# Three local edits in a fused feed-forward kernel: a sigmoid built from a tangent, one subtraction moved two products back, and the last additions cut in halves

## The chip, the cores and the metric

The kernel runs on one core of a Trainium2 chip, as one launch. The metric is device time in microseconds (us). Three runs of the kernel before took 884.63, 884.65 and 885.28 us (median 884.65).

Names used throughout: PE is the matrix engine (PEld its weight load), ACT the scalar engine, DVE the vector engine, POOL the engine that runs the remaining elementwise work, SP the engine whose queue issues nearly all transfers.

## The reference, cut to what matters

The input is 4096 tokens of 128 features. Layer 0 is a conditional mixture of experts followed by an eight-expert gated feed-forward; layer 1 is a second mixture (two shared experts, eight routed ones of which each token uses two) followed by a low-rank feed-forward. The change lies in layer 1 and in the last addition:

```python
# routing of layer 1, the "second choice" for half of the tokens
s = sigmoid(router_in @ W_router.T)              # tokens x 8
_, topk_idx = top_k(s + router_bias, 2)
denom = sum of s over the two chosen             # the "token sum"
gates = where(denom > 1e-9, s_sel / (denom + 1e-9), 0.5)
# routed experts
for e in range(8):
    h = gelu(x @ r_w1[e].T)                      # exact gelu
    routed += (h @ r_w2[e].T) * gates_full[:, e:e+1]
# low-rank feed-forward and residual
x = x + (gelu((x1 @ U1) @ V1 + b1) @ U2) @ V2 + b2
```

## The kernel before, in words

Tokens lie as eight blocks of 512 columns (b = 0 to 7), features across the 128 partitions. Every matrix product is made from a high part and a low part of its fp32 operands: the hidden value `Hf` is rounded to `HH` (fp32r), and `HL = Hf - HH` is the low part. A "down" product of a hidden tile takes one matmul with `HH` (line 973) and one with `HL` (line 975) in this part of the program.

The program is a list of items, one hidden tile of 128x512 each, walked by a slot number k. All engines are written out by hand in one loop over k, each in its own order; an item's "up" matmuls are issued in its slot and its "down" matmuls LAG = 5 slots later. In layer 1 the kinds are:

- S, a tile of a shared expert: six up matmuls (lines 933, 938, 952, two results), Silu on ACT into `Sg` (line 1087), product on DVE (line 1568);
- R, the routed expert `ex` of a block: three up matmuls, exact gelu in place in PSUM on ACT (line 1083), product with the token's gate on DVE (line 1575), which frees the PSUM bank;
- F, a tile of the low-rank feed-forward: one up matmul (line 908), gelu on ACT (line 1080).

Pairs of blocks are served together: S of both (8 tiles), F of the pair before (up to block 4), R of both (16 tiles). F of the blocks 5, 6 and 7 come last, behind R of block 7. Up results use four PSUM banks in turn; a matmul into a bank waits for what freed it four results ago.

In an R slot, rounding to `HH` is on ACT (line 1093), but on DVE for experts 3 and 7 (line 1585). The low part is on POOL (line 1683), but on DVE for experts 1 and 5 (line 1588), and for expert 7 of block 7. On DVE the product of slot k comes first and the rounding and the low part of the item of slot k-1 behind it. So the low part of expert 5 stands behind the product of expert 6.

The routing decision is `choose(g, step)`, spread over ten slots from `pick[g][0]` on; g = 1 (the second choice) starts at the first S tile of block 2, g = 0 earlier. In its first slot ACT takes the Sigmoid of `LR` (line 1047); DVE then finds the two largest of eight per token with 128x128 operations in PSUM and ends with sums, a reciprocal and two products (lines 1386 to 1404). PE transposes the result (line 878), DVE copies it (line 1407), SP writes it to `scratch`, and the gates of blocks 4 to 7 are read back from there.

At the end of a block ACT copies a PSUM result to `PH` (lines 1053, 1058), DVE makes `PS` (line 1545) or `QS` (line 1553) of it, PE multiplies `QS` by `V2S` (line 893), DVE adds bias and residual (line 1560), and SP sends the block out (line 748). Functions of ACT come in tables; a change of table is an instruction of its own, `ACT_TABLE_LOAD`.

## Time and profile before

| what | value |
|---|---|
| median of three runs | 884.65 us |
| the profiled execution | 884.92 us, its span 883.1 us |
| granted clock, mean over the span | 0.999 |
| PE busy | 869.6 us, 98% of the span |
| PEld, DVE, ACT, POOL busy | 78%, 77%, 65%, 46% |
| queue q1 (SP's transfers) | 82.15 MB, 30.4% of 16 engines' span |
| chain that ended last | PE 83%, DVE 6%, ACT 3%, issue 3% |

The span is from the first to the last record of the profiled execution; the rest of its 884.92 us lies around it. A row of the timeline gives the start, the duration, the engine with its line, the operation with what it writes and reads, and in brackets the idle time of the engine before it with what ended it. "x2" means two instructions merged.

### The profile page before, as it was taken

To read this page: it belongs to the slowest core of one execution; us is meant where nothing else is said; L and a number is where in the kernel's file an instruction comes from. 1 tells how busy PE (TensorE), PEld (TensorE's weight loads), DVE (VectorE), ACT (ScalarE), POOL (GpSimd) and SP (SyncE) were. 2 spreads that over 40 slices of the span, in tenths; PEclk is the share of its full clock that TensorE was granted. 3 is DMA by queue.
4 is the path that set the end of the run, shared out by engine and by line. 5 is a ranking of instruction groups with operands and counts; after the bars stand their busy time and mean duration, and the time that the engine had idled before them with its cause. 6 is when DMAs were issued, how large, how long until landed. Compare 5 with 4: busy or idle time off the path is not lost.

```text
span 883.1 us, 12612 instructions
## 1 busy us (share of the span) xinstructions
PE 869.6 (98%) x3838; PEld 691.1 (78%) x3838; DVE 678.7 (77%) x1091; ACT 573.8 (65%) x1031; POOL 407.5 (46%) x379
## 2 busy tenths in 40 slices
PE   9999999999999999999999999999999999999997
PEld 6788888777888888888888888888888887777773
DVE  7877777869689687686687686686665788998887
ACT  7888888765555455555555555555555678989795
POOL 7457783135356353252252252352324427755462
PEclk9999999999999999999999999999999999999999
DMA  9689880024113112012012012011010068482700
GB/s 313 223 277 312 290 296 32 1 86 135 49 48 111 36 48 84 1 47 84 1 49 83 1 49 84 0 48 49 1 47 1 1 131 201 99 174 56 159 25 36
DMA packets 36548, 83.23 MB, mean 94 GB/s; under 512 B 4480, under 2 KB 14592, under 8 KB 34688
## 3 DMA queue, kind: packets, MB, share of 16 engines
q1 hardware_dynamic: 36192, 82.15, 30.4%
q8 instruction: 31, 0.51, 0.2%
q14 instruction: 37, 0.30, 0.1%
q10 hardware_dynamic: 288, 0.26, 0.1%
HBM read 71.39 MB, written 6.83 MB: 89 GB/s over the span
## 4 chain that ended last, share of the span: by engine, by line
PE 83%; DVE 6%; ACT 3%; issue 3%; SPq 2%; DMA 2%; POOL 1%; DVEq 0%; ACTq 0%; POOLq 0%
PE ps L933 17%; PE ps L952 17%; PE ps L938 17%; PE ps L993 9%; PE ps L995 9%; PE ps L988 9%; DVE HL L1588 2%; SPq L658 1%; PE ps L975 1%; PE ps L973 1%; DMA TMP<-scratch 1%; DVE Hf L1575 1%; ACT HH L1093 1%; POOL HL L1683 1%; DVE Hf L1568 1%
## 5 line engine op out<-in xcount | busy, mean ns | idle before, releaser
L1087 ACT ACTIVATE Sg<-ps 128x512 f32<-128x512 f32 x288 | 171.7, 597 | 243.7 <-PE ps L952 243.1
L1568 DVE TENSOR_TENSOR Hf<-ps,Sg 128x512 f32<-128x512 f32 x288 | 198.0, 688 | 148.9 <-ACT Sg L1087 93.0
L1683 POOL TENSOR_TENSOR HL<-Hf,HH 128x512 fp32r<-128x512 f32 x135 | 181.1, 1348 | 170.4 <-ACT HH L1093 154.3
L1093 ACT ACTIVATE HH<-Hf 128x512 fp32r<-128x512 f32 x346 | 216.1, 625 | 19.0 <-DVE Hf L1568 12.7
L1588 DVE TENSOR_TENSOR HL<-Hf,HH 128x512 fp32r<-128x512 f32 x243 | 216.7, 892 | 4.4 <-ACT HH L1093 3.2
L933 PE MATMUL ps<-XHL,WBH 128*128 128x512 f32 x512 | 203.6, 398 | 1.6 <-DVE Hf L1568 1.5
L952 PE MATMUL ps<-XHL,WBH 128*128 128x512 f32 x512 | 202.1, 395 | 0.0
L938 PE MATMUL ps<-XHL,WBL 128*128 128x512 f32 x512 | 202.0, 395 | 0.0
L1698 POOL TENSOR_TENSOR XT<-XT,TMP 128x512 f32<-128x512 f32 x64 | 83.9, 1311 | 226.0 <-DVE TMP L1435 225.9
L933 PEld LDWEIGHTS ps<-XHL,WBH 128*128 128x128 f32 x512 | 96.0, 188 | 26.2 <-DVE Hf L1568 3.2
L952 PEld LDWEIGHTS ps<-XHL,WBH 128*128 128x128 f32 x512 | 96.0, 188 | 23.1
L938 PEld LDWEIGHTS ps<-XHL,WBL 128*128 128x128 f32 x512 | 96.2, 188 | 21.9
L993 PE MATMUL ps<-HH,WBL 128*128 128x512 f32 x256 | 101.0, 395 | 0.0
L988 PE MATMUL ps<-HH,WBH 128*128 128x512 f32 x256 | 100.7, 393 | 0.0
L995 PE MATMUL ps<-HL,WBH 128*128 128x512 f32 x256 | 100.7, 393 | 0.0
L1588 DVE TENSOR_TENSOR HL<-ps,HH 128x512 fp32r<-128x512 f32 (+1 forms) x116 | 69.7, 614 | 29.4 <-ACT HH L1093 28.3
L1080 ACT ACTIVATE ps<-ps,GWU 128x512 f32<-128x512 f32 (+1 forms) x84 | 49.2, 588 | 16.9 <-PE ps L952 16.8
L988 PEld LDWEIGHTS ps<-HH,WBH 128*128 128x128 f32 x256 | 48.0, 187 | 12.0 <-DVE TMP L1435 0.4
L993 PEld LDWEIGHTS ps<-HH,WBL 128*128 128x128 f32 x256 | 48.0, 188 | 11.8
L995 PEld LDWEIGHTS ps<-HL,WBH 128*128 128x128 f32 x256 | 48.1, 188 | 11.2
L933 PE MATMUL ps<-XHL,WCH 128*128 128x512 f32 x128 | 51.1, 399 | 1.2 <-ACT Sg L1087 0.8
L952 PE MATMUL ps<-XHL,WCH 128*128 128x512 f32 x128 | 50.5, 395 | 0.0
(261 smaller groups left out, 1327.8 us busy)
## 6 DMA issues: line engine op xcount, KB each, us to landing
CWB<-scratch SPq DMA_DIRECT2D x14, 1024.0 KB, 4.7
GWD<-expert_down SPq DMA_DIRECT2D x21, 576.5 KB, 4.5
GWU<-expert_up SPq DMA_DIRECT2D x21, 514.0 KB, 5.4
CWB<-scratch SPq DMA_DIRECT2D x40, 256.0 KB, 6.0
ST<-in_wb_dram SPq DMA_DIRECT2D x8, 768.0 KB, 6.6
ST<-scratch SPq DMA_DIRECT2D x24, 256.0 KB, 8.8
GX<-XT SPq DMA_DIRECT2D x68, 64.0 KB, 2.7
XT<-in_x_dram SPq DMA_DIRECT2D x8, 256.0 KB, 5.8
```

What stands on the lines that cost most here:

```text
L933: e.matmul(o, wh, tokens(it, 0), start=True, stop=False)
L938: e.matmul(o, wl, tokens(it, 0), start=False, stop=False)
L952: e.matmul(o, wh, tokens(it, 1), start=False, stop=True).then_inc(s_z, 1)
L988: e.matmul(bk[:, 0:n], wh, HH[:, hs, 0:n], start=it.new, stop=False)
L993: e.matmul(bk[:, 0:n], wl, HH[:, hs, 0:n], start=False, stop=False)
L995: e.matmul(bk[:, 0:n], wh, HL[:, hs, 0:n], start=False, stop=it.last).then_inc(s_down, 1)
L1087: e.activation(Sg[:, it.n % NG, :], zb[z % NZ][:, :], ACT.Silu).then_inc(s_act, 1)
L1093: e.activation(HH[:, it.n % NH, 0:it.cols], hidden_place(it), ACT.Copy).then_inc(s_hi_act, 1)
L1568: e.tensor_tensor(Hf[:, it.n % NS, :], zb[z % NZ][:, :], Sg[:, it.n % NG, :], ALU.mult).then_inc(s_prod, 1)
L1588: e.tensor_tensor(l, f, h.bitcast(F32), ALU.subtract).then_inc(s_lo_dve, 1)
L1683: e.tensor_tensor(HL[:, it.n % NH, :], Hf[:, it.n % NS, :], HH[:, it.n % NH, :].bitcast(F32), ALU.subtract).then_inc(s_lo_pool, 1)
L1698: e.tensor_tensor(XT[:, it.blk, :], XT[:, it.blk, :], TMP[:, t % 2, :], ALU.add).then_inc(s_acc, 1)
```

## The change

Four edits, all on ACT and DVE; PE, POOL and SP keep their instructions in their order.

1. The second choice's sigmoid is no longer one ACT instruction at the first S tile of block 2. ACT takes tanh(x/8) three slots earlier (`odds`), DVE makes 1/max(tanh+1, 1e-6) one slot later, ACT squares twice one slot after that, and DVE adds one and takes the reciprocal in the slot of that first S tile.
2. In both choices the token sum and two values made from it lie in PSUM (`total`, `above`) instead of the SBUF scratch `r0`, `r1`.
3. The low part of routed expert 5 (`low_after`) is written one slot later in DVE's order, behind the product of expert 7.
4. The last addition of block 6 is made in two halves of 256 columns, the first ahead of the last `QS`, the second in the old place.

```diff
+        odds = pick[1][0] - 3
+        y_half = {t_f[NBLK - 1] + 1: NBLK - 2}
...
+            it.low_after = it.kind == "R" and it.ex == 5 and not it.lo_pool
...
# ACT
+                if k == odds:
+                    e.wait_ge(*ab_done.of(("B", 7)))
+                    e.activation(pick_place(1)[0], LR[:, 16:32, 0:8], ACT.Tanh, scale=0.125).then_inc(s_odds, 1)
+                if k == odds + 2:
+                    e.wait_ge(s_score, 1)
+                    e.activation(pick_place(1)[1], pick_place(1)[0], ACT.Square, bias=1.0, scale=-2.0).then_inc(s_power, 1)
+                    e.wait_ge(s_power, 1)
+                    e.activation(pick_place(1)[0], pick_place(1)[1], ACT.Square).then_inc(s_power, 1)
...
# DVE, choose()
+                total, above = [ab_bank(("pick", g))[:, 384 + 16 * i:400 + 16 * i] for i in range(2)]
...
-                    link(e.tensor_reduce(r0[:, 0:16], sel, AX, ALU.add))
-                    after()
-                    link(e.tensor_scalar(r1[:, 0:16], r0[:, 0:16], 1e-9, None, ALU.add))
+                    link(e.tensor_reduce(total, sel, AX, ALU.add))
+                    after()
+                    link(e.tensor_scalar(above, total, 1e-9, None, ALU.add))
...
-                    link(e.tensor_tensor(r1[:, 0:16], r0[:, 0:16], r2[:, 0:16], ALU.mult))
+                    link(e.tensor_tensor(r1[:, 0:16], total, r2[:, 0:16], ALU.mult))
...
# DVE, the loop
+                if k == odds + 1:
+                    t = pick_place(1)[0]
+                    e.wait_ge(s_odds, 1)
+                    link(e.tensor_scalar(t, t, 1.0, 1e-6, ALU.add, ALU.max))
+                    after()
+                    e.reciprocal(t, t).then_inc(s_score, 1)
+                if k == odds + 3:
+                    t = pick_place(1)[0]
+                    e.wait_ge(s_power, 2)
+                    link(e.tensor_scalar(t, t, 1.0, None, ALU.add))
+                    after()
+                    link(e.reciprocal(t, t))
...
+                if k in y_half:
+                    b, c = y_half[k], slice(0, BLK // 2)
+                    e.wait_ge(*small.of(("y", b)))
+                    e.scalar_tensor_tensor(out=out_place(b)[:, c], in0=ab_bank(("y", b))[:, c], scalar=col("b2"),
+                                           in1=XT[:, b, c], op0=ALU.add, op1=ALU.add).then_inc(s_ab, 1)
...
+                if 2 <= k <= len(items) + 1 and items[k - 2].low_after:
+                    it = items[k - 2]
+                    e.wait_ge(*hi[it.n])
+                    e.tensor_tensor(HL[:, it.n % NH, :], hidden_place(it), HH[:, it.n % NH, :].bitcast(F32),
+                                    ALU.subtract).then_inc(s_lo_dve, 1)
...
-                    if not it.lo_pool:
+                    if not (it.lo_pool or it.low_after):
```

The order of ACT around the second choice, in block 1 (`ps<-ps` is a gelu, `ps<-LR` the sigmoid or the tanh). Before, from the copy to `PH` on:

```order
L1053 ACTIVATE PH<-ps 128x512
L1083 ACTIVATE ps<-ps 128x512
L1093 ACTIVATE HH<-Hf 128x512
L1083 ACTIVATE ps<-ps 128x512
L1093 ACTIVATE HH<-Hf 128x512
L1083 ACTIVATE ps<-ps 128x512
L1093 ACTIVATE HH<-Hf 128x512
L1047 ACT_TABLE_LOAD
L1047 ACTIVATE ps<-LR 128x128
L1087 ACT_TABLE_LOAD
L1087 ACTIVATE Sg<-ps 128x512 x2
```

In the changed kernel, from the gelu of expert 4 on:

```order
L1098 ACTIVATE ps<-ps 128x512
L1057 ACTIVATE ps<-LR 128x128
L1068 ACTIVATE PH<-ps 128x512
L1098 ACTIVATE ps<-ps 128x512
L1108 ACTIVATE HH<-Hf 128x512
L1098 ACTIVATE ps<-ps 128x512
L1108 ACTIVATE HH<-Hf 128x512
L1060 ACTIVATE ps<-ps 128x128
L1062 ACTIVATE ps<-ps 128x128
L1098 ACTIVATE ps<-ps 128x512
L1108 ACTIVATE HH<-Hf 128x512
L1102 ACT_TABLE_LOAD
```

The tanh stands ahead of the copy to `PH`, the two squares ahead of expert 7's gelu, and one of the two table loads is gone.

DVE at the same place (the `Hf` rows are the products of experts 5 to 7 of block 1 and of the first S tile; `HL` is the low part of expert 5, `HH` the rounding of expert 7). Before:

```order
L1545 SCALAR_TENSOR_TENSOR PS<-PH,sm,ps 128x512
L1575 TENSOR_TENSOR Hf<-ps,ST 128x512
L1575 TENSOR_TENSOR Hf<-ps,TMP 128x512
L1588 TENSOR_TENSOR HL<-Hf,HH 128x512
L1575 TENSOR_TENSOR Hf<-ps,TMP 128x512
L1568 TENSOR_TENSOR Hf<-ps,Sg 128x512
L1585 CAST HH<-Hf 128x512
```

Changed:

```order
L1575 SCALAR_TENSOR_TENSOR PS<-PH,sm,ps 128x512
L1611 TENSOR_TENSOR Hf<-ps,ST 128x512
L1520 TENSOR_SCALAR ps<-ps 128x128
L1522 RECIPROCAL ps<-ps 128x128
L1611 TENSOR_TENSOR Hf<-ps,TMP 128x512 x2
L1616 TENSOR_TENSOR HL<-Hf,HH 128x512
L1526 TENSOR_SCALAR ps<-ps 128x128
L1528 RECIPROCAL ps<-ps 128x128
L1604 TENSOR_TENSOR Hf<-ps,Sg 128x512
```

A reciprocal of 128x128 now stands ahead of the products of experts 6 and 7, another ahead of the first S tile's product, and `HL` between expert 7 and the second.

DVE behind block 7's expert 5, where F of block 5 begins. Before:

```order
L1575 TENSOR_TENSOR Hf<-ps,ST 128x512
L1575 TENSOR_TENSOR Hf<-ps,TMP 128x512
L1588 TENSOR_TENSOR HL<-Hf,HH 128x512
L1575 TENSOR_TENSOR Hf<-ps,TMP 128x512
L1585 CAST HH<-Hf 128x512
L1588 TENSOR_TENSOR HL<-Hf,HH 128x512
```

Changed:

```order
L1611 TENSOR_TENSOR Hf<-ps,ST 128x512
L1611 TENSOR_TENSOR Hf<-ps,TMP 128x512 x2
L1616 TENSOR_TENSOR HL<-Hf,HH 128x512
L1626 CAST HH<-Hf 128x512
L1629 TENSOR_TENSOR HL<-Hf,HH 128x512
```

The product of expert 7 has changed places with the low part of expert 5, which now stands directly ahead of expert 7's rounding.

## Rows read from the trace of the kernel before

**Rows 1.** The page: busy time, share of the span and instructions of each engine.

```profile
PE 869.6 (98%) x3838; PEld 691.1 (78%) x3838; DVE 678.7 (77%) x1091; ACT 573.8 (65%) x1031; POOL 407.5 (46%) x379
```

**Rows 2.** Timeline at the second choice's sigmoid, ACT, PE and DVE.

```profile
737.46 0.68 DVE L1575 TENSOR_TENSOR Hf<-ps,ST 128x512 f32<-128x512 f32 x1
...
738.71 0.58 ACT L1083 ACTIVATE ps<-ps 128x512 f32<-128x512 f32 x1
...
739.86 1.28 ACT L1047 ACT_TABLE_LOAD   x1
...
741.15 0.28 ACT L1047 ACTIVATE ps<-LR 128x128 f32<-128x128 f32 x1
...
742.23 0.40 PE L975 MATMUL ps<-HL,WD 128*128 128x512 f32 x1
742.75 1.09 ACT L1087 ACTIVATE Sg<-ps 128x512 f32<-128x512 f32 x2
...
743.40 0.50 PE L933 MATMUL ps<-XHL,WCH 128*128 128x512 f32 x1 [0.77 <-ACT Sg L1087]
```

**Rows 3.** DVE's groups by line and shape: busy us, mean ns | idle before.

```profile
L1321 DVE RECIPROCAL r<-r 128x32 f32<-128x32 f32 x2 | 0.7, 352 | 0.1
...
L1334 DVE RECIPROCAL r<-r 128x16 f32<-128x16 f32 x2 | 0.5, 252 | 0.1
```

**Rows 4.** Timeline, two places where a low part on DVE meets POOL's.

```profile
757.31 0.69 DVE L1588 TENSOR_TENSOR HL<-Hf,HH 128x512 fp32r<-128x512 f32 x1
...
757.41 1.73 POOL L1683 TENSOR_TENSOR HL<-Hf,HH 128x512 fp32r<-128x512 f32 x1 [1.24 <-ACT HH L1093]
...
804.76 1.29 POOL L1683 TENSOR_TENSOR HL<-Hf,HH 128x512 fp32r<-128x512 f32 x1 [0.26 <-ACT HH L1093]
...
804.83 1.78 DVE L1588 TENSOR_TENSOR HL<-Hf,HH 128x512 fp32r<-128x512 f32 x1
```

**Rows 5.** Timeline at the end of the second choice, DVE and PE.

```profile
753.47 1.14 DVE L1397 TENSOR_TENSOR r<-r 128x16 f32<-128x16 f32 x1
...
755.83 0.30 PE L878 MATMUL ps<-sm,q 128*128 128x128 f32 x1 [0.32 <-DVE q L1404]
...
759.20 0.50 PE L975 MATMUL ps<-HL,WD 128*128 128x512 f32 x1 [0.51 <-POOL HL L1683]
```

**Rows 6.** Timeline, end of block 6: gelu and rounding of expert 7.

```profile
852.76 0.58 ACT L1083 ACTIVATE ps<-ps 128x512 f32<-128x512 f32 x1
...
855.24 0.41 DVE L1585 CAST HH<-Hf 128x512 fp32r<-128x512 f32 x1
```

**Rows 7.** Timeline, end of block 3: from expert 7's gelu to the first Silu.

```profile
782.46 0.58 ACT L1083 ACTIVATE ps<-ps 128x512 f32<-128x512 f32 x1
...
783.66 1.29 POOL L1683 TENSOR_TENSOR HL<-Hf,HH 128x512 fp32r<-128x512 f32 x1 [0.40 <-ACT HH L1093]
...
783.74 0.68 DVE L1575 TENSOR_TENSOR Hf<-ps,TMP 128x512 f32<-128x512 f32 x1
...
784.47 0.51 PE L933 MATMUL ps<-XHL,WCH 128*128 128x512 f32 x1 [0.41 <-DVE Hf L1575]
...
784.90 0.60 ACT L1087 ACTIVATE Sg<-ps 128x512 f32<-128x512 f32 x1
```

**Rows 8.** Timeline, end of block 7: ACT, DVE and PE.

```profile
862.20 0.58 ACT L1083 ACTIVATE ps<-ps 128x512 f32<-128x512 f32 x1
...
864.18 0.80 DVE L1585 CAST HH<-Hf 128x512 fp32r<-128x512 f32 x1
...
866.84 0.50 PE L975 MATMUL ps<-HL,U2S 128*128 128x512 f32 x1
```

**Rows 9.** Timeline, the end: `QS` of block 7, last additions, their transfers.

```profile
877.49 0.75 DVE L1553 SCALAR_TENSOR_TENSOR QS<-PH,sm,ps 128x512 fp32r<-128x512 f32 x1 [0.98 <-ACT PH L1058]
878.15 1.48 DVE L1560 SCALAR_TENSOR_TENSOR Sg<-ps,sm,XT 128x512 f32<-128x512 f32 x2
...
878.92 1.98 SPq L748 DMA_DIRECT2D out_dram<-Sg  x2
```

More of the change, by code:

```diff
@@ L240, in build @@
         s_max = sem("s_max")
+        s_odds, s_power, s_score = sem("s_odds"), sem("s_power"), sem("s_score")
         s_gw, s_wr = sem("s_gw"), sem("s_wr")
@@ L299, in build @@
                 pick_at[t] = g, i
-        soft_b = {pick[g][0]: g for g in range(2)}
+        soft_b = {pick[0][0]: 0}
+        odds = pick[1][0] - 3
         turn_step = [6, 7]
@@ L356, in build @@
             if it.whole:
-                it.hi_act = it.lo_pool = False
+                it.hi_act = it.lo_pool = it.low_after = False
                 lo[it.n] = s_down, it.n + 1
@@ L453, in build @@
             for g in range(2):
-                if k == pick[g][0]:
+                if k == (odds if g else pick[0][0]):
                     ab_of["pick", g] = len(ab_of)
@@ L490, in build @@
                 ph.add(("Q", read_q[k]))
+                if read_q[k] == NBLK - 1:
+                    ab_done.add(("y half", NBLK - 2))
                 ab_done.add(("Q", read_q[k]))
@@ L1351, in choose @@
                 if k == 1:
-                    e.wait_ge(s_exp, 4 + g)
+                    if g == 0:
+                        e.wait_ge(s_exp, 4)
+                    after()
                     e.wait_ge(f_scr[g][1 - g], 16)
@@ L1385, in choose @@
                     after()
-                    link(e.tensor_reduce(r0[:, 0:16], sel, AX, ALU.add))
+                    link(e.tensor_reduce(total, sel, AX, ALU.add))
                     after()
-                    link(e.tensor_scalar(r1[:, 0:16], r0[:, 0:16], 1e-9, None, ALU.add))
+                    link(e.tensor_scalar(above, total, 1e-9, None, ALU.add))
                 if k == 6:
                     after()
-                    link(e.reciprocal(r2[:, 0:16], r1[:, 0:16]))
-                    link(e.tensor_scalar(r0[:, 0:16], r0[:, 0:16], 1e-9, None, ALU.is_gt))
+                    link(e.reciprocal(r2[:, 0:16], above))
+                    link(e.tensor_scalar(total, total, 1e-9, None, ALU.is_gt))
                     after()
-                    link(e.tensor_scalar(r0[:, 16:32], r0[:, 0:16], -0.5, 0.5, ALU.mult, ALU.add))
+                    link(e.tensor_scalar(r0[:, 0:16], total, -0.5, 0.5, ALU.mult, ALU.add))
                 if k == 7:
                     after()
-                    link(e.tensor_tensor(r1[:, 0:16], r0[:, 0:16], r2[:, 0:16], ALU.mult))
+                    link(e.tensor_tensor(r1[:, 0:16], total, r2[:, 0:16], ALU.mult))
                     after()
@@ L1400, in choose @@
                     after()
-                    link(e.tensor_tensor(sel, sel, bc(r0[:, 16:32], 2, s3), ALU.add))
+                    link(e.tensor_tensor(sel, sel, bc(r0[:, 0:16], 2, s3), ALU.add))
                     after()
@@ L1559, in vector_program @@
                         e.wait_ge(f_out[b - 2], 16)
-                    e.scalar_tensor_tensor(out=out_place(b), in0=ab_bank(("y", b))[:, :], scalar=col("b2"),
-                                           in1=XT[:, b, :], op0=ALU.add, op1=ALU.add).then_inc(s_ab, 1)
+                    c = slice(BLK // 2 if b == NBLK - 2 else 0, BLK)
+                    e.scalar_tensor_tensor(out=out_place(b)[:, c], in0=ab_bank(("y", b))[:, c], scalar=col("b2"),
+                                           in1=XT[:, b, c], op0=ALU.add, op1=ALU.add).then_inc(s_ab, 1)
                 if k < len(items) and items[k] and items[k].kind in "BS":
```

## The prediction

> **What bounds the kernel now.** I read the page first: PE is busy for 98% of the span [rows 1], 869.6 us over 3838 instructions, so 0.23 us each. What an edit on ACT or DVE can give or take is only what PE waits for, or what lies behind its last matmul. Next I read the waits of PE: all of some weight falls behind 740 us, in layer 1. Then I read the timeline at each such place: the first Silu after the second choice [rows 2], the transposition of its result [rows 5], the end of an odd block of routed experts [rows 7], the end of block 7 [rows 8] and the end of the program [rows 9]. In each group the reader is to see which engine PE waits for, and then what that engine itself had been held by: in the routed blocks it is mostly DVE, whose instructions follow each other with no gap, and DVE is held by POOL [rows 4]. The sum is made against the profiled execution, 884.92 us (span 883.1, 1.8 around it); that is 0.27 above the median of the runs, so I add the sum to 884.65.
>
> **Edit 1, the sigmoid.** Before, a load (1.28), the sigmoid (0.28) and a second load stand ahead of the first Silu, which starts at 742.75. PE issued its last matmul at 742.23, could have gone on at 742.46, and went on at 743.40 [rows 2]: 0.94 lost. The change takes away 1.28 + 0.28, with small gaps 1.59, ahead of that Silu.
>
> What comes in: a tanh of the same shape as the sigmoid, three slots earlier (0.28, ahead of a gelu that waited for PE anyway), and two squares of about 0.28 each ahead of expert 7's gelu, which wait for the first reciprocal on DVE. The reciprocals are the price. No 128x128 reciprocal stands in the trace, so I go by the two that do: 32 elements took 352 ns and 16 took 252 [rows 3], 6.25 ns per element; 128 elements then take 0.352 + 96 x 0.00625 = 0.95 us. The lower bound is what the sigmoid of that shape took, 0.28, the upper 1.1. I take 0.95, since the slope comes from the same instruction.
>
> The Trainium skill (VectorE: DVE Perf Modes, section "First, the fixed hardware budget") says why a reciprocal is unlike other operations: it divides iteratively, with a repeat count of 8. By the clock that the Trainium skill gives (SBUF — State Buffer, section "SBUF: two separate sides"), 0.96 GHz, that is an estimate of 1.07 us for 128 elements, and the sum would be 0.1 us higher.
>
> Expert 5's product ends at 738.14 [rows 2]. Add (0.3) and reciprocal (0.95) end at 739.4. The squares, one waiting for the other, end at 739.95. Expert 7's gelu starts there and not at 738.71: 1.24 later. The first Silu starts at 742.75 + 1.24 - 1.59 = 742.40, ends at 743.0, and PE goes on at 743.05: **0.35 gained of 0.94**. The second reciprocal stands ahead of the first S product, which then starts about 743.1 and is done when PE wants its bank at 743.8, if the low part of expert 5, now between the two, does not wait for POOL (edit 3). If it does, it ends near 743.0, the reciprocal near 744.3, the product near 744.95, and PE goes on there at 745.0 in place of 744.2: 0.8 to 0.9 lost. Bounds of edit 1: -0.94 to +0.9.
>
> **Edit 2, sums in PSUM.** Line 1397 multiplies 16 numbers per partition in SBUF and took 1.14 us [rows 5], because POOL was at work. With an operand in PSUM I expect under 0.2. The chain to the transposition is then 1 us shorter, and the 0.49 that PE loses ahead of it (755.83 in place of 755.34, where the matmul before it ended its turn) goes. But the next wait takes its place: at 759.20 [rows 5] PE waits for a low part on POOL which follows a rounding on ACT, which stands behind a table load and the first gelu of F. None of these waits for the choice. PE comes there 0.49 earlier and waits 0.49 longer. I take 0; bounds -0.49 to 0.
>
> **Edit 3, the low part of expert 5.** Let g be the start of expert 7's gelu. The product of expert 7 can start at g + 0.61, and what follows it on DVE at g + 1.21 (an instruction starts some 0.08 before the end of the one ahead [rows 9]). POOL starts the low part of expert 6 at g + 1.20: 782.46 and 783.66 [rows 7]. Both read two tensors in SBUF. What happens then [rows 4] shows: DVE 0.10 ahead took 0.69, and POOL 1.73 (ending 1.83 after DVE's start); POOL 0.07 ahead took 1.29, and DVE 1.78, ending 0.56 after POOL. So one waits for the other in full. Before the change DVE did the low part ahead of the product and met the POOL operation before.
>
> The Trainium skill (SBUF — State Buffer, section "Who interferes with whom") has this as a lock: the one that issues first holds the second pair of ports for its whole instruction. The rows agree to 0.1 us. The rule speaks against the edit: it moves the low part from one POOL operation onto the start of the next.
>
> Even blocks. I take DVE to be first. POOL's low part then ends at g + 1.21 + 1.83 = g + 3.04, and the rounding of expert 7 on DVE (also a user of SBUF alone: 864.18 to 864.98, 0.28 behind POOL's end [rows 8]) ends at g + 3.32. Before it ended at 855.65 with g = 852.76 [rows 6], g + 2.89. DVE is **0.43 late** at the start of the odd block, and has no gap in blocks 3, 5 and 7 to make it up. In block 1 I take the gaps before it to absorb it.
>
> Ends of blocks 3 and 5. There PE waits for expert 7's product, 784.47 [rows 7], where it could have been 0.57 earlier. The product would be done at g + 1.29 = 783.75, and that wait goes. But the next bank waits for the first Silu, which ends at 785.50 and hangs on ACT's chain, not on the product; before, PE reached it at 784.47 + 0.34 + 4 x 0.23 = 785.73. With ACT's chain 0.43 late behind DVE, PE reaches it at 786.0: 0.25 lost. The same three instructions stand at the end of block 5, so **0.5 for both**. Without the lateness it would be a gain of 0.2 to 0.3.
>
> End of block 7. Here F follows, with only three matmuls per slot, and the low parts of experts 5 and 7 and of F's first tile follow each other on DVE up to PE's wait at 866.84 [rows 8]. POOL's operation ends at 862.20 + 1.20 + 1.30 = 864.70 and the rounding of expert 7 at 864.98. The low part of expert 5 lay ahead of this; now it lies behind or inside it, and its 0.55 comes on top, whoever is first. With the lateness from block 6: 0.43 + 0.55 = **1.0 lost**. From 866.84 on PE has hardly a wait, so nothing gives it back. Bounds of edit 3: -0.5 to +2.2.
>
> **Edit 4, the halves.** DVE sits idle for 0.98 ahead of the last `QS` [rows 9]. Half an addition, some 0.45, fits in, or makes `QS` late by up to 0.1. The second half ends 0.2 to 0.3 sooner than the whole did. Block 7's own addition gains nothing: it waits for the matmul, which is done when the first addition ends. But the two transfers were issued within 1.98 us, the first at 878.92 though the second's data was ready at 879.63 [rows 9], so the second issue seems held by the first. I take -0.15, bounds -0.3 to +0.1.
>
> **Sum:** -0.35 + 0 + 0.5 + 1.0 - 0.15 = +1.0. I take off 0.1 for small waits that shrink: 884.65 + 0.9 = **885.5 us**.
>
> **The rivals.**
> - *The product ahead pays.* The reciprocals cost little (0.3) and ACT's chain is not late: PE goes on at 742.46 (-0.94), blocks 3 and 5 give 0.3, block 7 comes out even, the end gives 0.15: -1.4, 883.25 us. For it: PE's waits in [rows 2] and [rows 7] are just what the edits aim at. Against it: the slope of [rows 3] and the order at block 7.
> - *POOL is first (slower).* The start of the low part of expert 5 and of POOL's differ by 0.01 in my reckoning. If POOL wins, DVE waits until g + 3.06. In block 1 this puts the second reciprocal behind it: +0.85. In block 6 it makes DVE 1.1 late in place of 0.43: +0.7 at the end. With the rest, +0.85 + 0.5 + 1.7 - 0.15 = +2.9, 887.5 us. It decides from the point where POOL starts before DVE, as in [rows 4]; it needs both places.
> - *Hidden.* DVE's lateness is absorbed by short gaps, the waits merely change their names, and what is gained at 743 is lost at 867: 884.4 to 884.9 us. For it: 759.20 shows that one wait replaces another.
>
> **How the numbers follow.** Forecast 0.42, the product pays 0.2, POOL first 0.15, hidden 0.23. 0.2% is 1.8 us, about what a measurement of this kernel can tell from no change. Most of the cases lie within it: the first rival passes it only with the wait of edit 2 on top (0.05), the second mostly does, and the forecast hardly ever (together 0.15). The range reaches to the first rival's time, 883.2, and short of the second's, 887.2.
>
> **What the profile after would show.** Right: two 128x128 reciprocals of 0.9 to 1.0 us; PE's wait at the first Silu down to about 0.6; line 1397's successor under 0.2 us and a longer wait for POOL near 759; expert 7's rounding at the end of even blocks 0.4 later after its gelu; PE's matmul for the first F tile of block 5 about a microsecond later against the end of block 6; both last transfers issued a little sooner. Wrong: reciprocals near 0.3 us; no wait on POOL in the low part of expert 5 at the end of block 7; a stretch from 850 to 870 that is as long as before.

## The result and the profile after

The changed kernel took 887.72 us (median of 6 runs, 887.59 to 888.21) against 884.64 (6 runs): ratio 1.0035, 95% interval 1.0025 to 1.0045. It is slower by 3.1 us. The forecast was 885.5 us, and its range ended at 887.2. The profiled execution took 887.80 us; its span is 885.9, which is 2.8 more than that of before.

The page of the changed kernel, beside [rows 1]:

```profile
PE 870.8 (98%) x3838; PEld 690.2 (78%) x3838; DVE 681.8 (77%) x1096; ACT 573.2 (65%) x1032; POOL 410.2 (46%) x379
```

PE's work is the same, so I compare the starts of the same matmul in both traces. Each line of the table gives what the changed kernel lost (+) or gained (-) over one stretch. That PE "loses" time at a matmul means in this whole document that its start is further from the one ahead of it than before; the idle time in brackets in its row is some 0.17 shorter than that loss.

| stretch (matmul at its end, before and after) | difference | predicted |
|---|---|---|
| start to 300.65 / 301.28 | +0.63 | 0 |
| to the second S matmul, 744.20 / 746.45 | +1.62 | -0.35 |
| to 801.38 / 803.99 (block 3) | +0.36 | +0.25 |
| to 847.59 / 850.45 (block 5) | +0.25 | +0.25 |
| to 866.84 / 870.69 (block 7) | +0.99 | +1.0 |
| to the last matmul, 878.38 / 882.17 | -0.06 | 0 |
| to the end of the span, 883.1 / 885.9 | -0.99 | -0.15 |

Blocks 3, 5 and 7 came out at the size that was forecast. The second line did not. The first line lies ahead of every edit, and the last one belongs to that one execution of before (see edit 4 below); the five lines between them add up to +3.16, near the +3.1 of the medians.

The moved low part on DVE and POOL's low part of expert 6 both hang on expert 7's gelu and come up almost together. I call that a race: the one that is first wins, and the other waits until it is done. Timeline of the changed kernel, end of block 0, POOL and DVE (columns: start, us, engine, line), and then PE:

```profile
731.11 1.29 POOL L1724 TENSOR_TENSOR HL<-Hf,HH 128x512 fp32r<-128x512 f32 x1 [0.38 <-ACT HH L1108]
731.13 1.82 DVE L1616 TENSOR_TENSOR HL<-Hf,HH 128x512 fp32r<-128x512 f32 x1
732.87 0.68 DVE L1611 TENSOR_TENSOR Hf<-ps,ST 128x512 f32<-128x512 f32 x1
...
741.71 0.50 PE L939 MATMUL ps<-XHL,WCH 128*128 128x512 f32 x1 [0.29 <-DVE Hf L1611]
...
742.93 0.50 PE L939 MATMUL ps<-XHL,WCH 128*128 128x512 f32 x1 [0.26 <-DVE Hf L1611]
```

L1616 is the moved low part of expert 5. POOL's low part starts 0.02 ahead of it, and DVE waits until POOL is done: 1.82 in place of 0.68. In the kernel before, the product `Hf` stood at 731.15 and is now at 732.87: 1.72 later, 1.1 of it beyond the offset of 0.63. Nothing makes this up: with the two PE rows and the matmul behind each, still ahead of the first Silu's, PE has lost 1.09.

And at the second choice, which answers to [rows 2]:

```profile
742.71 1.28 ACT L1102 ACT_TABLE_LOAD   x1
742.77 1.28 POOL L1724 TENSOR_TENSOR HL<-Hf,HH 128x512 fp32r<-128x512 f32 x1 [1.52 <-ACT HH L1108]
742.80 1.81 DVE L1616 TENSOR_TENSOR HL<-Hf,HH 128x512 fp32r<-128x512 f32 x1
...
744.65 0.50 PE L939 MATMUL ps<-XHL,WCH 128*128 128x512 f32 x1 [0.29 <-ACT Sg L1102]
744.85 0.97 DVE L1528 RECIPROCAL ps<-ps 128x128 f32<-128x128 f32 x1
745.72 0.67 DVE L1604 TENSOR_TENSOR Hf<-ps,Sg 128x512 f32<-128x512 f32 x1
746.45 0.50 PE L939 MATMUL ps<-XHL,WCH 128*128 128x512 f32 x1 [0.83 <-DVE Hf L1604]
```

POOL is first again, by 0.03. The second reciprocal and the first S product stand behind the low part, and PE loses 1.0 at 746.45. At the first Silu it now waits 0.29 in place of 0.77; the forecast had it shrink too, by 0.35.

The low part of expert 5 was not always late. At the end of block 6 DVE had only 0.01 against it and won:

```profile
856.82 1.87 POOL L1724 TENSOR_TENSOR HL<-Hf,HH 128x512 fp32r<-128x512 f32 x1 [0.40 <-ACT HH L1108]
...
856.83 0.68 DVE L1616 TENSOR_TENSOR HL<-Hf,HH 128x512 fp32r<-128x512 f32 x1
```

### The profile page after: what moved, and what is told of

Its sections match the earlier page's. It is cut to its first block, busy times and chain, and to the rows that moved or that the text cites. A ratio compares the mean times of both kernels' runs of the same rounds, so it can differ in the third digit from the quotient of the medians.

```text
span 885.9 us, 12618 instructions
## 1 busy us (share of the span) xinstructions
PE 870.8 (98%) x3838; PEld 690.2 (78%) x3838; DVE 681.8 (77%) x1096; ACT 573.2 (65%) x1032; POOL 410.2 (46%) x379
## 4 chain that ended last, share of the span: by engine, by line
PE 84%; DVE 8%; ACT 3%; issue 3%; DMA 1%; POOL 1%; SPq 0%; DVEq 0%; ACTq 0%; POOLq 0%
PE ps L939 18%; PE ps L958 17%; PE ps L944 17%; PE ps L999 9%; PE ps L1001 9%; PE ps L994 9%; DVE HL L1629 2%; PE ps L981 2%; DVE Hf L1611 1%; PE ps L979 1%; ACT HH L1108 1%; DVE HH L1626 1%; DVE Hf L1604 1%; ACT ps L1098 1%; DMA XT<-in_x_dram 1%
## 5 line engine op out<-in xcount | busy, mean ns | idle before, releaser
L1724 POOL TENSOR_TENSOR HL<-Hf,HH 128x512 fp32r<-128x512 f32 x135 | 184.1, 1371 | 170.2 <-ACT HH L1108 154.7
L1629 DVE TENSOR_TENSOR HL<-Hf,HH 128x512 fp32r<-128x512 f32 x235 | 208.1, 886 | 3.9 <-ACT HH L1108 3.2
L944 PE MATMUL ps<-XHL,WBL 128*128 128x512 f32 x512 | 202.0, 395 | 0.0
```

What stands on the lines that cost most here:

```text
L944: e.matmul(o, wl, tokens(it, 0), start=False, stop=False)
L1629: e.tensor_tensor(l, f, h.bitcast(F32), ALU.subtract).then_inc(s_lo_dve, 1)
L1724: e.tensor_tensor(HL[:, it.n % NH, :], Hf[:, it.n % NS, :], HH[:, it.n % NH, :].bitcast(F32), ALU.subtract).then_inc(s_lo_pool, 1)
```

## The experiments

"Before" in a comparison is the kernel before on the same chip, 884.6 to 884.8 each time (21 to 29 runs). A median of about ten runs is known to 0.8 us here.

**One edit at a time.** Each of the four alone; the first is the changed kernel with the other three undone, the others are the kernel before with one edit.

```diff
 # e1_sigmoid, against the changed kernel
-            it.low_after = it.kind == "R" and it.ex == 5 and not it.lo_pool
+            it.low_after = it.kind == "R" and False
 ...           (sums back in r0, r1; last additions whole)
 # e2_low, e3_halves, e4_sums, against the kernel before
+            it.low_after = it.kind == "R" and it.ex == 5 and not it.lo_pool
+        y_half = {t_f[NBLK - 1] + 1: NBLK - 2}
+                total, above = [ab_bank(("pick", g))[:, 384 + 16 * i:400 + 16 * i] for i in range(2)]
 ...           (and the lines that use them, as in the change)
```

> The sigmoid of the second choice from the tangent, and nothing else of the change: the low part of expert 5 stays ahead of expert 7's product, the sums of the choice stay in SBUF, the last addition is whole. The theory, from the two traces (edits 1 and 3 cost together at the first Silu of the second choice, since the second reciprocal stands behind a low part that waited for POOL): with the low part back in its old place DVE isn't held by POOL between the first Silu and the first S product, and the step is what the prediction reckoned for it, -0.35 us, so 884.3; the matmuls from 746 to 800 us lie 0.3 us earlier than before, and PE's largest loss there is about 0.6 instead of 0.94. The rival (the two reciprocals, 1.9 us on a DVE that has no gap, cost by themselves): +0.9 to +1.6 us, so 885.5 to 886.2, with PE losing about 0.8 at the first S product in this kernel too.

> The kernel before with only the low part of expert 5 moved behind expert 7's product, in all eight blocks; the sigmoid is the old one. The theory (as predicted: DVE 0.43 late behind even blocks, 0.25 at the ends of blocks 3 and 5 each, 1.0 at the end of block 7): +1.5 us, so 886.1, and at the end of block 1, where no reciprocal stands behind it, nothing or up to 0.4. The rival (the losses seen at the block ends in the changed kernel come from elsewhere, as from the start that lay 0.6 later): under +0.5 us, and PE's offset against before doesn't grow by 1.0 between 850 and 868 us.

> The kernel before with only the last additions in halves. The theory (half an addition fits into DVE's idle time ahead of the last QS, so the second half ends 0.2 to 0.3 sooner): -0.15 us, 884.5. The rival by the changed kernel's trace, in which the stretch from the last matmul to the end was 1.0 shorter: -1.0 us, 883.7. A third: the 1.0 belongs to the issue of the two last transfers (1.98 us for two before, 1.34 for two after) and not to the halves; then the profile shows the issue at either length whatever the additions do, and the time is 884.5 to 884.7.

> The kernel before with only the token sums of the choice in PSUM (both choices). The theory (the next wait, for the low part on POOL near 759 us, takes the place of the one removed): 0, so 884.6, with PE's wait ahead of the transposition gone and the one near 759 us longer by 0.5. The rival (the choice's chain sets the time): -0.5 us, 884.15. That it costs: up to +0.3, if one of the sums' instructions in PSUM takes longer than in SBUF.

Measured: the sigmoid 884.18 (ratio 0.9994, 0.9986 to 1.0003), the low part 888.04 (1.0036, 1.0023 to 1.0048), the halves 884.48 (0.9998, 0.9989 to 1.0007), the sums 884.89 (1.0000, 0.9991 to 1.0008). Against 884.69 that is -0.5, +3.35, -0.2 and +0.2: only edit 3 loses. My theory of it was too small (+1.5), and the rival, under 0.5, is out. That the four add up to +2.85, near the whole, is in part chance. The trace of edit 3 alone lost the race at block 0 and won it at block 1, and PE's clock fell in it; the trace of the changed kernel lost both races, and its clock did not fall.

With the sigmoid alone, PE at the first Silu, then with the sums alone, PE at the place of [rows 5]:

```profile
742.95 0.50 PE L936 MATMUL ps<-XHL,WCH 128*128 128x512 f32 x1 [0.29 <-ACT Sg L1099]
```
```profile
759.24 0.50 PE L975 MATMUL ps<-HL,WD 128*128 128x512 f32 x1 [1.03 <-POOL HL L1684]
```

The first is 0.45 earlier than 743.40 (forecast 743.05). The second shows the wait of 0.51 grown to 1.03 in the place of the one removed.

With the low part alone, POOL won at block 0 by 0.02 (731.03 against 731.05, 1.81), and PE went on at the first Silu 1.65 later than before, 1.09 of it beyond this trace's offset of 0.56, behind a wait of 1.84. Behind it:

```profile
745.05 0.53 PE L934 MATMUL ps<-XHL,WCH 128*128 128x512 f32 x1 [1.84 <-ACT Sg L1088]
745.38 0.62 PE L939 MATMUL ps<-XHL,WCL 128*128 128x512 f32 x1
745.80 0.63 PE L953 MATMUL ps<-XHL,WCH 128*128 128x512 f32 x1
...
748.78 0.41 PE L939 MATMUL ps<-XHL,WCL 128*128 128x512 f32 x1
749.03 0.39 PE L953 MATMUL ps<-XHL,WCH 128*128 128x512 f32 x1
```

From 745.38 to 748.78 the matmuls come 0.41 to 0.43 apart in place of 0.23. By windows the same stretch is (columns: window, its length, PE busy, granted clock, DMA share, GB/s):

```profile
738.00:743.00 5.00, 5.00 (x23) 1.00 0.87 211
743.00:746.00 3.00, 1.16 (x4) 0.90 0.98 160
746.00:750.00 4.00, 4.00 (x13) 0.65 0.91 279
750.00:754.00 4.00, 4.00 (x19) 1.00 0.76 163
```

PE waited, its granted clock fell to the lower of its two levels, 1.2 GHz, and came back. That cost eight distances of 0.19 more each, 1.5 us. The six runs of this kernel form two groups: 886.57, 887.07 and 887.19 us with a mean granted clock of 0.999 or 1.0, and 888.88, 888.93 and 889.52 with 0.997. So the 888.04 lies between a time with the fall and one without.

**Which block's low part.** The set of blocks in which it is moved:

```diff
-            it.low_after = it.kind == "R" and it.ex == 5 and not it.lo_pool
+            it.low_after = it.kind == "R" and it.ex == 5 and it.blk != 0 and not it.lo_pool   # f1_but0, f3_low_but0
+            it.low_after = it.kind == "R" and it.ex == 5 and it.blk > 1 and not it.lo_pool    # f2_but01
+            it.low_after = it.kind == "R" and it.ex == 5 and it.blk in (3, 5) and not it.lo_pool  # f4_low35
```

> The changed kernel with the low part of expert 5 in block 0 back ahead of the product; in blocks 1 to 7 it stays behind it. The theory, from the eight places of that low part in the changed kernel and in the one with edit 3 alone: at the end of block 0 POOL starts 0.02 ahead of DVE, the low part takes 1.81 in place of 0.68, and DVE is 1.07 late at the first Silu; so 887.72 - 1.07 = 886.65. If the 1.81 at block 1 (POOL 0.03 ahead) is only a consequence of that lateness, PE's loss of 1.0 at the first S product goes too, and the time is 885.6 to 885.8. The rival (the lateness behind block 0 is made up before block 1, as the prediction took it, and what is lost near 744 us comes from the two reciprocals): 887.4 to 887.8.

> The changed kernel with the low part of expert 5 back ahead of the product in blocks 0 and 1; in blocks 2 to 7 it stays behind it. The theory (the losses beyond the forecast are the two places where POOL starts first, both in blocks 0 and 1, and all other terms hold): the forecast's own time, 884.65 - 0.5 for the sigmoid + 0.5 for the ends of blocks 3 and 5 + 1.0 for block 7 - 0.2 for the halves = 885.45, and PE's loss at the first Silu about 0.46, none at the first S product. The rival (start, reciprocals or PSUM sums carry the loss): 886.5 or more.

> The kernel before with the low part of expert 5 behind the product in blocks 1 to 7, not in block 0. Edit 3 alone cost 3.35 us, its runs lay between 886.57 and 889.52, and its trace shows PE's granted clock at 0.65 from 746 to 750 us, behind a wait of 2.01 us. The theory (block 0's 1.07 makes that wait long, and the clock falls behind it in about half of the runs, 1.8 us each time): without block 0 the wait is 0.94 again, the clock stays at 1.0, the runs lie within 1.3 us of each other, and the median is 886.1, the prediction's +1.5. The rival without the clock: 888.04 - 1.07 = 887.0, and the runs spread as before.

> The kernel before with the low part of expert 5 behind the product only in blocks 3 and 5. The theory (at those ends the move itself gains 0.2 to 0.3, since PE's wait for expert 7's product goes, and what costs is the 0.43 by which DVE comes late from the even block ahead): 884.65 - 0.5 = 884.15, PE's loss of 0.57 at the end of block 3 goes or is under 0.3, and the matmuls behind 790 us lie earlier than before. The rival (the moved low part costs at these places itself, through POOL): +0.3 to +0.5, 885.0 to 885.2.

Measured: 886.87 (1.0027, 1.0017 to 1.0038), 886.0 (1.0019, 1.001 to 1.0028), 886.98 (1.0027, 1.0017 to 1.0036), 884.44 (1.0000, 0.9991 to 1.0009). The first is where the theory put it, with block 1 lost still (742.05 against 742.08), so that loss is no consequence of block 0; its trace has blocks 5 to 7 lost as well, which the theory did not have. The second came 0.5 above the theory and the third 0.9. Their traces say why: with block 0 right, other places were lost. DVE stood 0.01 to 0.02 behind POOL at blocks 3, 5, 6 and 7 of the second kernel and lost all four; at blocks 6 and 7 of the third. With both lost, PE loses 0.83 at the end of block 6 and 1.44 at that of block 7, in all 0.6 more than with both won, and in both traces the clock fell behind the second, which cost another 1.4 to the last matmul. My forecast that the runs of the third would lie within 1.3 us failed: they lie between 885.62 and 888.21. The fourth gained 0.17, below what can be told; in its trace block 3 gave nothing and block 5 0.08 against the kernel before, so the prediction's "gain of 0.2 to 0.3" without the lateness was too much.

**Deciding the race.** The same changed kernel, once with a small instruction ahead of POOL's low part of expert 6, once with one ahead of DVE's low part of expert 5; without edit 3; and once more as it is.

```diff
+        tiny = sb("tiny", [P, NBLK])
 # g1_dve_first: POOL, behind the wait and ahead of the low part of expert 6
+                    if it.kind == "R" and it.ex == 6:
+                        e.memset(tiny[:, it.blk:it.blk + 1], 0.0)
 # g2_pool_first: DVE, behind the wait and ahead of the low part of expert 5
+                    e.tensor_copy(tiny[:, it.blk:it.blk + 1], col("b2"))
 # g3_no_low
+            it.low_after = it.kind == "R" and False
```

> The changed kernel, with one more instruction on POOL: a write of one element per partition, behind the wait and ahead of the low part of expert 6, in each block. It delays POOL's low part by its own time, so DVE's low part of expert 5 is first at all eight places; nothing is taken away. The theory (which of the two starts first decides, and all that the change costs beyond the forecast is two lost races, in blocks 0 and 1): the low part takes 0.7 to 0.8 at all eight places, 1.07 and 1.0 come back, and the time is 885.5 to 885.9 although an instruction was added. The rival (the order of the start is only a sign of something else, as DMA traffic or the reciprocals): 887.7 or more.

> The changed kernel, with one more instruction on DVE: a copy of one element per partition, ahead of the low part of expert 5, in each block. POOL's low part of expert 6 is then first at all eight places. The theory: the low part of expert 5 takes 1.8 wherever POOL's operation was met at its start; to the losses of blocks 0 and 1 come those of blocks 3 and 5 to 7, 0.5 to 0.8 each where DVE has no gap, and PE's wait at the end of block 7 passes 1.4, behind which the clock may fall (1.8): 889.0 to 891. The rival (no race, POOL and DVE share what they use): within 0.5 of the changed kernel, 887.5 to 888.3.

> The changed kernel without edit 3: the sigmoid from the tangent, the sums in PSUM, the halves. The theory (the three add up as measured alone, -0.5, 0 to +0.2 and -0.2): 884.0. The rival by the trace of the changed kernel, where the second reciprocal lay ahead of the first S product: 885.0 or more, with a loss of PE over 0.5 at that product.

> The changed kernel, unchanged, profiled once more. In its first profile the matmuls lay 0.63 later than before from the first 10 us on, where nothing was changed; profiles of other kernels lay between -0.15 and +0.75 there. If that is the chance of a single execution, this profile shows another offset; if it belongs to the program, 0.6 again. The races in blocks 0 and 1, 0.02 apart, are shown a second time: if they are chance, one of the eight goes the other way.

Measured: DVE first 885.2 (1.0006, 0.9997 to 1.0015), POOL first 888.09 (1.004, 1.0026 to 1.0054), without edit 3 883.93 (0.9994, 0.9985 to 1.0003), unchanged 889.66 (two runs, 889.23 and 890.1). Block 0 of the first and of the second kernel:

```profile
730.30 0.10 POOL L1726 MEMSET tiny<- 128x1 f32 x1 [0.36 <-ACT HH L1109]
730.35 0.68 DVE L1617 TENSOR_TENSOR HL<-Hf,HH 128x512 fp32r<-128x512 f32 x1
730.36 1.83 POOL L1727 TENSOR_TENSOR HL<-Hf,HH 128x512 fp32r<-128x512 f32 x1
730.94 0.68 DVE L1612 TENSOR_TENSOR Hf<-ps,ST 128x512 f32<-128x512 f32 x1
```
```profile
730.56 1.29 POOL L1726 TENSOR_TENSOR HL<-Hf,HH 128x512 fp32r<-128x512 f32 x1 [0.38 <-ACT HH L1109]
730.58 0.14 DVE L1617 COPY tiny<-sm 128x1 f32<-128x1 f32 x1
730.64 1.76 DVE L1618 TENSOR_TENSOR HL<-Hf,HH 128x512 fp32r<-128x512 f32 x1
732.32 0.68 DVE L1612 TENSOR_TENSOR Hf<-ps,ST 128x512 f32<-128x512 f32 x1
```

An instruction of 0.10 us per block more, and the low part takes 0.68 at all eight places. With a copy of 0.14 on DVE instead it takes 1.74 to 1.77 at six of them; at blocks 2 and 4 DVE is 0.15 ahead all the same and wins. The time of the second was forecast at 889 to 891 and came at 888.09: its clock did not fall in the profiled execution, and the idle tile `tiny` is worth 1.0 (below).

The changed kernel taken again lost the race at blocks 0 and 1, as the first time, and at blocks 6 and 7 too, where it had won. So the change costs 3.1 us in one set of runs and 5.0 in another:

```profile
856.78 1.29 POOL L1724 TENSOR_TENSOR HL<-Hf,HH 128x512 fp32r<-128x512 f32 x1 [0.40 <-ACT HH L1108]
856.79 1.82 DVE L1616 TENSOR_TENSOR HL<-Hf,HH 128x512 fp32r<-128x512 f32 x1
```

Its profiled execution took 890.1, that is 2.3 more than the first one of the same program: 0.6 for blocks 6 and 7, 1.4 for the clock, which fell behind the wait of 1.27 at 869.18, and 0.3 outside the span:

```profile
869.18 0.51 PE L981 MATMUL ps<-HL,WD 128*128 128x512 f32 x1 [1.27 <-DVE HL L1616]
...
869.76 0.63 PE L979 MATMUL ps<-HH,WD 128*128 128x512 f32 x1
870.19 0.63 PE L981 MATMUL ps<-HL,WD 128*128 128x512 f32 x1
```

The thirteen traces with the moved low part have it at 75 places. By the timeline's starts, which are rounded to 0.01, the races look like a matter of chance: of 37 places at which DVE stands 0.01 or 0.02 behind, 20 were won by DVE and 17 by POOL. The traces hold the starts in nanoseconds, and there the two cases separate:

| DVE behind POOL, ns | places | DVE first (0.68 us) | POOL first (1.74 to 1.83 us) |
|---|---|---|---|
| -249 to -7 | 27 | 27 | 0 |
| +7 to +15 | 18 | 18 | 0 |
| +16 | 4 | 2 | 2 |
| +17 to +33 | 20 | 0 | 20 |
| +76 to +91 | 6 | 0 | 6 |

So the theory that the order of the start decides holds, with the border at 16 ns behind by these stamps and not at 0; why it lies there no run shows. What changes from one execution to the next is on which side of the border a start falls. In the changed kernel DVE was 11 ns behind at block 6 in the first profile and won, and 18 ns behind in the second and lost.

Without edit 3 the time was the sum of the three others: 883.93 against 884.0 forecast, and PE lost nothing at the first S product.

**What was left open**: the price of the reciprocals, the division of block 7's term, and a version of the best parts.

```diff
 # h1_half (edit 3 off): in place of tanh(x/8), two squares and two reciprocals
+                    e.activation(pick_place(1)[0], LR[:, 16:32, 0:8], ACT.Tanh, scale=0.5).then_inc(s_odds, 1)
+                    link(e.tensor_scalar(t, t, 0.5, 0.5, ALU.mult, ALU.add))
 # h2_best: h1_half, and the low part moved in blocks 3 and 5, with the write on POOL there
+            it.low_after = it.kind == "R" and it.ex == 5 and it.blk in (3, 5) and not it.lo_pool
 # h3_low7: the kernel before, and the low part moved in block 7, with the write on POOL there
```

> The changed kernel without edit 3, and the sigmoid taken as half of one plus the tangent of half the argument: the two squares and both reciprocals go, one tanh and one operation of DVE are left. The theory (as the prediction had it, the first reciprocal makes expert 7's gelu 1.16 late, 739.87 in place of 738.71, and that is what is left of PE's wait at the first Silu): the wait of 0.45 there is gone or under 0.1, and the time is that of the kernel without edit 3, 883.93, less 0.4: 883.5. The rival (what is left of the wait there belongs to the table load, or a next wait takes its place, as at 759 us): 883.8 to 884.1.

> What the runs point to: the sigmoid without reciprocals, the sums in PSUM, the halves, the low part of expert 5 behind the product only in blocks 3 and 5, and there a write of one element per partition on POOL, ahead of its low part, so that DVE is first. The theory: 883.5 for the kernel without edit 3 and with the short sigmoid, less 0.1 to 0.2 that the low part in blocks 3 and 5 alone gave: 883.3. The rival (nothing beyond the sigmoid is worth anything): 883.5 to 883.9.

> The kernel before with the low part of expert 5 behind the product only in block 7, with the one-element write on POOL ahead of its low part there, so that DVE is first and comes on time from block 6. The theory (the prediction's term for block 7 is 0.55 for the low part that comes on top, and 0.43 for the lateness from block 6): +0.55, 885.2, and from 850 to 868 us PE's offset grows by 0.5 to 0.6. The rival (the whole 1.0 belongs to block 7 itself): +1.0, 885.65.

Measured: 883.76 (0.9985, 0.9976 to 0.9994), 882.25 (0.9972, 0.9962 to 0.9982), 884.3 (0.9994, 0.9985 to 1.0003), all against 884.84. In the first the wait at the first Silu is gone, Silu starting at 741.79 in place of 742.75, and from the matmul near 301 to the one that waits for POOL near 759 it needs 457.49 in place of 458.14: the rest of the wait was the reciprocals' price, as the theory had it. In the median 0.17 of it is seen, which is within the noise.

The other two were faster than forecast, where nothing in them was changed. From the matmul near 301 us to the first Silu's, the kernel before needs 442.75 and h3_low7, with the same wait at its end, 442.07. All kernels with the tile `tiny` showed this, and it had to be taken apart:

```diff
 # i1_tile, against the kernel before; i2_after_tile, against the changed kernel
         LR = sb("LR", [P, NB, 16])
+        tiny = sb("tiny", [P, NBLK])
 # i3_best_plain: h2_best without the tile and without the write on POOL
```

> The kernel before with a tile of 8 numbers per partition more in SBUF, which nothing reads or writes; it moves all tiles behind it by 32 bytes. The theory (the matmuls from 301 to 743 us come 0.3 ns closer, as in all four kernels that had this tile, whatever else was in them): 884.7 - 0.7 to 1.0 = 883.7 to 884.0, and 442.1 us from the matmul near 301 to the one near 743 in place of 442.75. The rival (the tiny instruction or chance): 884.7.

> The changed kernel with the same idle tile and no other instruction: the control of the run in which POOL was delayed and the time came to 885.2. The theory (the race costs 1.07 + 1.0 in blocks 0 and 1 and more where blocks 6 and 7 are lost too, the tile gives 0.7 to 1.0): 886.8 to 888.2, so at least 1.6 above 885.2. The rival (the tile was what the delayed kernel gained from): 885.2 to 885.8.

> The version that the runs point to without the tile and without the write on POOL: short sigmoid, sums, halves, low part behind the product in blocks 3 and 5, where the race is left to chance. The theory: 883.76 for the kernel without edit 3 and with the short sigmoid, less 0.1 to 0.2: 883.6. The rival (the 882.25 came from the order in blocks 3 and 5): 882.5 or less.

Measured: 883.71 (0.9989, 0.998 to 0.9998), 886.94 (1.0024, 1.0015 to 1.0033), 883.89 (0.9988, 0.9979 to 0.9997), all against 884.76. A tile that nothing reads gives 1.05 (by its interval, 0.2 to 1.8). The page of the kernel with it (line, group, busy and mean ns); the same line before had 202.0 and 395:

```profile
L939 PE MATMUL ps<-XHL,WBL 128*128 128x512 f32 x512 | 200.9, 392 | 0.0
```

So the race has its control: 886.94 with the tile alone, five of eight races lost in its trace, and 885.2 with the tile and the write on POOL, all eight won. That is 1.7 for one instruction per block. Against the kernel before with the same tile (883.71), the changed kernel with every race won is still 1.5 slower; without the tile it would stand near 886.2, an estimate from 885.2 and 1.05. The plain version came 0.3 above its theory, both races won in its trace. The version with tile and write is 1.6 faster than it, 0.6 more than the tile gave. The other 0.6 is not explained; each of the two medians is known to 0.8.

Block 7, DVE first and on time. The kernel with the moved low part needs 19.73 from the matmul at 846.95 to the one at 866.68, the kernel before 19.25: +0.48, where the prediction had 0.55 for the low part, and the changed kernel +0.99 with the lateness. In the medians it is +0.6, when the kernel before with the same tile is the base (884.3 against 883.71).

## Why the prediction was wrong

**The step that failed** is in edit 3: "Even blocks. I take DVE to be first", and "In block 1 I take the gaps before it to absorb it". POOL was first at block 0, by 0.02, and nothing absorbed it: 1.09 lost ahead of the first Silu. At block 1 POOL was first by 0.03, which is worth 1.0 with the second reciprocal behind it. Together 2.1, against 0. Even with DVE first at all eight places block 0 is not free: in the trace with the write on POOL, PE loses 0.47 at 741.52 and the matmul behind it. That is the lateness of 0.43 that I had put at nothing, and it is why the changed kernel with every race won would still stand near 886.2 and not at 885.5.

The chance was misread as well. I had the two starts 0.01 apart in my own reckoning (g + 1.20 and g + 1.21) and still gave POOL's win 0.15, and tied it to blocks 1 and 6 both. In the changed kernel POOL starts at g + 1.19 to 1.21 and DVE at g + 1.22 to 1.23 at blocks 0, 1 and 3, and 0.01 is as much as decides here. With six such places (blocks 2 and 4 stand apart), to lose none is the unlikely case. The rival's mechanism was the right one, and its place for a loss of 0.85 at block 1 too (measured 1.0). That its 887.5 lies so near the measured 887.72 is luck: its second place, block 6, was won in the first profile, and block 0, which I had not looked at, lost 1.09 in its stead.

**Edit 1**, -0.35: right. Alone it gave -0.45 in the trace and -0.5 in the runs (interval -1.2 to +0.3). The reciprocals of 128x128 were priced at 0.95 from the slope of [rows 3] and took:

```profile
L1522 DVE RECIPROCAL ps<-ps 128x128 f32<-128x128 f32 x1 | 1.0, 967 | 0.0
L1528 DVE RECIPROCAL ps<-ps 128x128 f32<-128x128 f32 x1 | 1.0, 966 | 0.0
```

The estimate of 1.07 that went by the Trainium skill (VectorE: DVE Perf Modes, section "First, the fixed hardware budget") is 0.1 too high. The sentence on what happens if the low part waits for POOL was also right: 0.8 to 0.9 lost at the first S product, 1.0 measured.

**Edit 2**, 0: right. The product is down from 1.14 to 0.17, the wait ahead of the transposition is gone, and the next wait takes its place:

```profile
755.86 0.17 DVE L1415 TENSOR_TENSOR r<-ps,r 128x16 f32<-128x16 f32 x1
```
```profile
761.50 0.50 PE L981 MATMUL ps<-HL,WD 128*128 128x512 f32 x1 [1.01 <-POOL HL L1724]
```

**Edit 3, the ends of blocks 3, 5 and 7**, +0.25, +0.25, +1.0: +0.36, +0.25, +0.99, with the waits under the names that were forecast ([rows 7] against 788.19, `0.30 <-ACT Sg`). For block 7 place and size are as reckoned. For blocks 3 and 5 the reason is only half shown. In blocks 2 and 4 DVE started 0.20 ahead of POOL, not behind, and the lateness came by POOL's later end. At the end of block 5 the lateness acts where the prediction had it: PE gains 0.28 at the product and loses 0.52 at the first Silu. In block 3 it cost PE 0.31 near 780, a place that the prediction does not name, and at the block's end 0.64 went and 0.57 came back at the first Silu. That the two sum up to +0.25 there is luck, since without any lateness the end of block 3 looks the same: with the low part moved in blocks 3 and 5 alone, PE waits 0.31 for the first Silu at 785.44. The gain there was 0 and 0.08, not 0.2 to 0.3.

The Trainium skill (SBUF — State Buffer, section "Who interferes with whom") gives the rule that the first to issue holds the ports for its whole instruction. By that rule, the trace agrees but for the 16 ns: 71 of 75 places go by the order of the start with the border there, and the other four lie on it. The rule was cited, and its consequence for a tie was not drawn.

**Edit 4**, -0.15: nothing. DVE does the half in its idle time, as forecast:

```profile
880.88 0.48 DVE L1581 SCALAR_TENSOR_TENSOR Sg<-ps,sm,XT 128x256 f32<-128x256 f32 x1 [0.58 <-PE ps L899]
881.28 0.74 DVE L1588 SCALAR_TENSOR_TENSOR QS<-PH,sm,ps 128x512 fp32r<-128x512 f32 x1
881.95 0.48 DVE L1596 SCALAR_TENSOR_TENSOR Sg<-ps,sm,XT 128x256 f32<-128x256 f32 x1
...
882.45 1.34 SPq L754 DMA_DIRECT2D out_dram<-Sg  x2
882.68 0.75 DVE L1596 SCALAR_TENSOR_TENSOR Sg<-ps,sm,XT 128x512 f32<-128x512 f32 x1 [0.26 <-PE ps L899]
```

The transfer of block 6 is issued 0.28 behind the start of the last matmul in place of 0.54. But block 7's own addition ends 1.26 behind that start, as before (1.25), and the two issues together end 1.62 behind it with halves and with whole additions: they take 1.34 in all twelve traces with halves, and 1.07 or 1.08 in seven of the eight with whole additions. From the last matmul's start to the end of the last record it is 3.77 or 3.78 in six of these eight traces and 3.75 to 3.77 in ten of the twelve with halves: a gain of 0.01. The other four, 4.3 to 5.1, are of both kinds, and the profile of before, 4.76, is one of them. So the -0.99 of the table is that execution and not the halves, and so is the 1.98 of [rows 9] from which the prediction argued.

**The start**, +0.63, isn't settled. In the trace after, DVE's cast stands 0.02 behind POOL at the start and waits for it, where before it was 0.09 ahead with 0.42:

```profile
6.61 1.30 POOL L1640 TENSOR_TENSOR WAS<-ST,WAS 128x512 fp32r<-128x512 f32 x1 [4.04 <-ACT WAS L1013]
6.63 1.56 DVE L1466 CAST XHL<-XT 128x512 fp32r<-128x512 f32 x1
```

The second profile of the changed kernel showed 0.62 again, there with a wait for the first transfers. In the six traces in which this cast starts behind POOL, PE is 0.5 to 0.8 later than before at 27 us. Of the thirteen others eleven are within 0.2 of before, and two are 0.45 and 0.47 later. So the late start goes with the order at this place, which no edit touches. At the matmul near 301 us the other 18 traces lie between -0.14 and +0.99. That the offset differs by the program can't be excluded.

## What to carry to other kernels

Where two engines that exclude each other hang on the same instruction of a third, look at every place at which they meet and not at two. If the starts are within 0.02 us, take each place as one that can be lost, or make the order certain: here an instruction of 0.10 us ahead of the operation that is to wait was worth 1.7 us. Then price a long wait of TensorE twice, once for itself and once for the clock that can fall behind it. A gain of under 1 us needs a control, since moving the tiles gives as much: the best version, 882.25 (0.9972, 0.9962 to 0.9982 of before; 5.5 us below the changed kernel), has 1.05 from an idle tile, and 0.6 that is not explained.

## What the runs showed of the hardware

- Exclusion by a hair. Of DVE and POOL, each with a subtraction of two SBUF tensors of 128x512, the later one takes 1.74 to 1.87 for an operation that takes 0.68 or 1.29 alone, where the starts lie within 0.1. By the nanoseconds of 13 traces DVE was first in 45 of 45 places up to 15 ns behind, and POOL in 26 of 26 from 17 ns on. The side changes between executions of one program.
- PE's clock fell to 1.2 GHz behind a wait of PE of 1.84 (one trace) and of 1.27 or 1.28 (three traces), in the 11 us ahead of which PE had stood idle for 0.67, 0.18 and 0.28. Behind the same idle times, within 0.02, and waits of 1.26 to 1.28 it stayed at 2.4 GHz in three other traces, so these waits alone do not decide it. Where it fell it cost 1.4 to 1.5.
- A new tile of 32 bytes per partition, ahead of others, brought the starts of the 1919 matmuls from 301 to 743 us, where PE never waits before the last, 0.34 ns closer on average, 0.66 in all, and 1.05 in the medians. Not all of them: matmuls of line 938 (939 with the tile) came down from 395 to 392 ns, those of line 933 (934) went up from 398 to 399. What in the addresses does it was not tried.
